# One of eight parts of a depthwise convolution made by ScalarE and GpSimd instead of VectorE, and one input projection issued earlier on TensorE

## What is computed

```python
hs = rmsnorm(hidden_states, ln_in_w)                 # 1024 tokens x 256
x, z = split(hs @ in_proj_w.T)                       # 512 channels each
xc = silu(depthwise_conv1d(x, conv_w, taps=4) + conv_b)
dt, Bm, Cm = split(xc @ x_proj_w.T, [128, 144])      # the "small" projection, 160 columns
dt = softplus(rmsnorm(dt) @ dt_proj_w.T + dt_proj_b)
# then a scan over the tokens: h = h * exp(dt * A) + dt * xc * B ;  y = sum(h * C)
```

## Time and profile before

| | us |
|---|---|
| median of 3 runs | 632.63 (631.25 to 633.44) |
| the profiled execution, its own time | 633.35 |
| its span, first to last instruction | 631.6 |
| busy PE / DVE / ACT / POOL | 587.5 / 467.1 / 387.2 / 300.3 |
| granted TensorE clock, mean | 0.988 |

### The profile page before, as it was taken

The page is one execution under the profiler, slowest core; times in us unless marked ns, Lnnn a source line. Parts: engine busy times, 40 slices in busy tenths (PEclk is TensorE's granted clock), DMA queues, the critical chain, the costliest instruction groups (busy, mean ns, idle before and its releaser), DMA issues.

```text
span 631.6 us, 10934 instructions
## 1 busy us (share of the span) xinstructions
PE 587.5 (93%) x3641; PEld 444.4 (70%) x3641; DVE 467.1 (74%) x788; ACT 387.2 (61%) x882; POOL 300.3 (48%) x242
## 2 busy tenths in 40 slices
PE   6999689998999999999999999999999999998874
PEld 3554589887998887597779779778855555665542
DVE  6989999999999967535463543553655789998885
ACT  5689899999999956522241231321755664687543
POOL 7022699999999991223333434344012332225101
PEclk9999899999999999999999999999999999999898
DMA  8001641211211117424440450411700000000002
GB/s 285 3 2 45 208 186 51 59 59 51 59 59 51 35 40 302 155 92 175 169 177 28 172 182 26 173 38 30 274 1 1 1 2 0 1 1 1 2 0 67
DMA packets 18261, 51.50 MB, mean 82 GB/s; under 512 B 3842, under 2 KB 9603, under 8 KB 16548
## 3 DMA queue, kind: packets, MB, share of 16 engines
q1 hardware_dynamic: 15172, 41.43, 18.5%
q0 software_dynamic: 2752, 7.34, 3.9%
q10 hardware_dynamic: 288, 2.10, 0.9%
HBM read 46.21 MB, written 4.66 MB: 81 GB/s over the span
## 4 chain that ended last, share of the span: by engine, by line
PE 67%; ACT 13%; DVE 10%; issue 5%; DMA 4%; SPq 0%; POOL 0%; POOLq 0%; DVEq 0%; ACTq 0%
PE ps L2174 11%; PE ps L2247 8%; ACT arena L689 7%; PE ps L2182 6%; PE ps L2236 4%; PE ps L2268 4%; ACT arena L704 3%; PE ps L1957 3%; PE ps L1942 3%; PE ps L1991 2%; PE ps L1783 2%; PE ps L2197 2%; PE ps L1792 2%; PE ps L1944 2%; DVE arena L1304 2%
## 5 line engine op out<-in xcount | busy, mean ns | idle before, releaser
L460 POOL TENSOR_TENSOR arena<-arena 128x1024 f32<-128x1024 f32 x63 | 147.3, 2393 | 3.4 <-DVE arena L1304 3.0
L1304 DVE TENSOR_TENSOR_SCAN arena<-arena,ps 128x1024 f32<-128x1024 f32 x64 | 143.4, 2279 | 4.0 <-ACT arena L689 0.9
L689 ACT ACTIVATE arena<-arena,a_neg 128x510 f32<-128x510 f32 x128 | 84.6, 710 | 1.9 <-DVE arena L1304 1.9
L2174 PEld LDWEIGHTS ps<-arena 128*128 128x128 f32 x660 | 75.5, 192 | 3.9 <-issue 3.1
L2174 PE MATMUL ps<-arena 128*128 128x128 f32 x660 | 77.2, 277 | 0.3 <-DVE arena L1481 0.3
L1942 PE MATMUL ps<-ident,arena 128*128 128x128 f32 x384 | 64.7, 278 | 9.9 <-ACT arena L700 8.6
L1957 PE MATMUL ps<-ident,arena 128*128 128x128 f32 x512 | 67.3, 274 | 2.5 <-DVE arena L1313 1.8
L900 ACT ACTIVATE arena<-ps 128x256 f32<-128x256 f32 x45 | 17.2, 383 | 83.0 <-PE ps L2174 83.0
L704 ACT ACTIVATE arena<-arena,b_tok 128x512 f32<-128x512 f32 x96 | 64.8, 710 | 0.0
L1957 PEld LDWEIGHTS ps<-ident,arena 128*128 128x128 f32 x512 | 57.8, 141 | 4.0 <-DVE arena L1313 1.3
L2247 PE MATMUL ps<-arena 128*128 128x512 f32 x128 | 58.2, 595 | 0.0
(11 more groups left out here) (317 smaller groups left out, 1147.2 us busy)
## 6 DMA issues: line engine op xcount, KB each, us to landing
arena<-in_w_moe SPq DMA_DIRECT2D x8, 2176.0 KB, 9.1
arena<-c_dram SPq DMA_DIRECT2D x32, 256.0 KB, 3.1
arena<-in_w_o ACTq DMA_DIRECT2D x1, 2048.0 KB, 12.7
arena<-in_w_qT SPq DMA_DIRECT2D x1, 2048.0 KB, 11.0
arena<-moe_out SPq DMA_DIRECT2D x8, 256.0 KB, 4.7
arena<-in_w_q SPq DMA_DIRECT2D x1, 2048.0 KB, 10.2
x<-in_x SPq DMA_DIRECT2D x2, 512.0 KB, 4.7
arena<-in_w_in SPq DMA_DIRECT2D x2, 512.0 KB, 6.5
```

The lines of the kernel that those rows point to most:

```text
L460: pool.tensor_tensor(in_chunks(hC[unit % 3]), in_chunks(h[unit % 3]), c_bc[:, m % C_BUFS, :].unsqueeze(1).to_broadcast([P, 2, HALF]), ALU. ...
L689: ins = nc.scalar.activation(dA_b[:, unit % 2, 2 * k:2 * k + 2, 1:], dt_b[:, c, 2 * half:2 * half + 2, 1:], ACT.Exp, scale=a_neg[:, c, n:n ...
L1304: nc.vector.tensor_tensor_scan(h[unit % 3], dA[:, k, :], ps[:, 2 * k:2 * k + 2, :].rearrange("p a b -> p (a b)"), 0.0, ALU.mult, ALU.add). ...
L2174: ins = nc.tensor.matmul(ps[:, bank, c * P:(c + 1) * P], w13[:, k, chunk * P:(chunk + 1) * P], xT[:, k, :], start=(k == 0), stop=(k == KD ...
```

## The change

Part (2, 0) of the convolution is taken out of DVE's list. ACT makes its four products instead (`multiply_taps`: Identity with the tap as a scale, three behind `take_in(2, 0)` and one behind `take_in(3, 0)`) into a new tile `tap_products`, which lies where the scan's rows `c_bc` are loaded later. POOL adds them up in three adds, between `negate_rates` and `rstd_of_dt(0)`, and ACT's `convolved(2, 0)` reads the sum. The last two chunks of the first half change places (3 before 2), for the Silu and for `project_small`. On PE `project_in(3, 1)` goes ahead of the four `project_small(., 0)`. On ACT `take_counts` goes ahead of the first `take_in`, `take_x(1)` ahead of `take_in(2, 0)`, and `take_in(3, 1)` ahead of `squares_of_small(0)`. Two semaphores are merged into one to make room for the new one, with the same waits.

```diff
+        tap_products = view(104.5, [TAPS, HALF])
-        CONV_TURNS = (((0, 0),), ((1, 0),), ((2, 0), (3, 0)), ((0, 1), (1, 1)), ((2, 1), (3, 1)))
+        CONV_TURNS = (((0, 0),), ((1, 0),), ((3, 0),), ((0, 1), (1, 1)), ((2, 1), (3, 1)))
+        SUMMED = (2, 0)
+        CHUNKS = ((0, 1, 3, 2), (0, 1, 2, 3))
+        convolved_at = lambda c, half: CI * half + CHUNKS[half].index(c) + 1
-        X_TAKEN, COUNTS_TAKEN = (1, 2), 3
+        X_TAKEN, COUNTS_TAKEN = (1, 3), 2
             negate_rates()
+            for k in range(1, TAPS):
+                pool.wait_ge(s["tap_products"], TAPS + k - 1)
+                pool.tensor_tensor(tap_products[:, 0, :], tap_products[:, 0, :], tap_products[:, k, :], ALU.add).then_inc(s["tap_products"], 1)
             rstd_of_dt(0)
+            def multiply_taps(*taps):
+                c, half = SUMMED
+                act.wait_ge(s["in_out"], CI * half + c + 1)
+                for k in taps:
+                    nc.scalar.activation(tap_products[:, k, :].rearrange("p (b t) -> p b t", b=2), xpad[:, c, 2 * half:2 * half + 2, k:k + SEQ], ACT.Identity,
+                                         scale=lane[:, c, LANE_AT["conv_w"] + k:LANE_AT["conv_w"] + k + 1]).then_inc(s["tap_products"], 1)
             def convolved(c, half):
-                act.wait_ge(s["conv_acc"], tap_added(c, half, TAPS - 1))
-                nc.scalar.activation(xc[:, c, halves[half]], conv[:, c, :], ACT.Silu,
+                if (c, half) == SUMMED:
+                    act.wait_ge(s["tap_products"], 2 * TAPS - 1)
+                else:
+                    act.wait_ge(s["conv_acc"], tap_added(c, half, TAPS - 1))
+                src = tap_products[:, 0, :] if (c, half) == SUMMED else conv[:, c, :]
+                nc.scalar.activation(xc[:, c, halves[half]], src, ACT.Silu,
             masks()
+            take_counts()
             take_in(0, 0)
             take_in(1, 0)
+            take_x(1)
             take_in(2, 0)
-            take_x(1)
+            multiply_taps(0, 1, 2)
             take_in(3, 0)
-            take_counts()
+            multiply_taps(3)
+            take_in(0, 1)
             convolved(0, 0)
-            take_in(0, 1)
             take_in(1, 1)
             convolved(1, 0)
             take_in(2, 1)
+            convolved(3, 0)
             convolved(2, 0)
-            convolved(3, 0)
+            take_in(3, 1)
             squares_of_small(0)
             take_small(0)
-            take_in(3, 1)
             convolved(0, 1)
             project_in(2, 1)
+            project_in(3, 1)
             project_small(0, 0)
             project_small(1, 0)
+            project_small(3, 0)
             project_small(2, 0)
-            project_small(3, 0)
-            project_in(3, 1)
             route_out()
             transpose_dt(0)
```

More of the change, by code:

```diff
@@ L228, in build @@
             gathered1 gathered2 gathered3 xT_psum xT_done gu_psum gate_act hid_done y_psum y_ready y_stored x1_sum waited
-            bn3 eps3 rstd_x1 x_normed ld_v ld_o ld_kq kv_psum kv_out k_squared
+            bn_x eps3 rstd_x1 x_normed ld_v ld_o ld_kq kv_psum kv_out k_squared
             k_ms masked k_rstd k_normed x1T_psum x1T_done q_psum q_squared q_eps q_rstd s_psum s_taken
             s_shifted s_exp s_soft pT_psum pT_done attn_psum attn_taken eps4 rstd_x2 ld_idx ld_late gathered_w0
-            gathered_w1 iota_done counted spread_psum spread_done quantised wT_psum wT_done x_scaled x_size_ready x_quant
+            gathered_w1 tap_products iota_done counted spread_psum spread_done quantised wT_psum wT_done x_scaled x_size_ready x_quant
             xT8_psum xT8_done ff_psum ff_read ff_gate ff_in t_scaled t_in_ready t_size_ready prod_done t_done t_psum
-            tT_done y2_psum y2_read bn5 eps5 rstd_out early_out out_shift stored""".split()
+            tT_done y2_psum y2_read eps5 rstd_out early_out out_shift stored""".split()
         s = {n: sem(n) for n in names}
@@ L1117, in convolve @@
                     if half:
-                        dve.wait_ge(s["conv_out"], c + 1)
+                        dve.wait_ge(s["conv_out"], convolved_at(c, 0))
                 for k in range(TAPS):
@@ L1200, in scan_inputs @@
                 dve.wait_ge(s["softplus"], n + 1)
-                dve.wait_ge(s["conv_out"], n + 1)
+                dve.wait_ge(s["conv_out"], convolved_at(c, half))
                 nc.vector.tensor_tensor(dtx[half][:, c, :], dt[:, c, halves[half]], xc[:, c, halves[half]], ALU.mult).then_inc(s["dtx_done"], 1)
@@ L1496, in variances @@
             def variances(stats, eps, tiles):
-                dve.wait_ge(s[stats], tiles.stop)
+                dve.wait_ge(s["bn_x"], stats + tiles.stop)
                 for i in range(tiles.start, tiles.stop):
@@ L1519, in add_results @@
                     dve.wait_ge(s["x1_sum"], 2 * part + i + 3)
-                    nc.vector.bn_stats(bn[:, i, :], x[:, i, :]).then_inc(s["bn3"], 1)
+                    nc.vector.bn_stats(bn[:, i, :], x[:, i, :]).then_inc(s["bn_x"], 1)
             def take_result_half(half):
@@ L1527, in _ @@
             add_results(1)
-            variances("bn3", "eps3", half_tiles[0])
+            variances(0, "eps3", half_tiles[0])
             add_results(2)
@@ L1533, in _ @@
             add_results(3)
-            variances("bn3", "eps3", half_tiles[1])
+            variances(0, "eps3", half_tiles[1])
             dve.wait_ge(s["rstd_x1"], 2)
@@ L1632, in add_result @@
                 dve.wait_ge(s["y2_read"], t + 1)
-                nc.vector.bn_stats(bn[:, t, :], x[:, t, :]).then_inc(s["bn5"], 1)
+                nc.vector.bn_stats(bn[:, t, :], x[:, t, :]).then_inc(s["bn_x"], 1)
             take_scores(0)
@@ L1731, in _ @@
             scale_of_hidden(7)
-            variances("bn5", "eps5", OUT_PARTS[0])
+            variances(TILES, "eps5", OUT_PARTS[0])
             add_result(6)
@@ L1737, in _ @@
             round_hidden(7)
-            variances("bn5", "eps5", OUT_PARTS[1])
+            variances(TILES, "eps5", OUT_PARTS[1])
             dve.wait_ge(s["rstd_out"], 2)
@@ L1741, in _ @@
             add_result(7)
-            variances("bn5", "eps5", OUT_PARTS[2])
+            variances(TILES, "eps5", OUT_PARTS[2])
             dve.wait_ge(s["rstd_out"], 3)
@@ L1800, in project_small @@
                         pe.wait_ge(s["routes_out"], 1)
-                pe.wait_ge(s["conv_out"], CI * half + c + 1)
+                pe.wait_ge(s["conv_out"], convolved_at(c, half))
                 for i in range(HALF_TILES):
@@ L1804, in project_small @@
                     ins = nc.tensor.matmul(ps[:, 2 * half + i // 2, (i % 2) * D:(i % 2) * D + XP], xc[:, c, tile * P:(tile + 1) * P], w_x[:, c, :],
-                                           start=(c == 0 and i % 2 == 0), stop=(c == CI - 1), skip_group_check=True)
+                                           start=(c == 0 and i % 2 == 0), stop=(c == CHUNKS[half][-1]), skip_group_check=True)
                 ins.then_inc(s["xproj_psum"], 1)
```

## The result

The changed kernel takes 635.06 us, median of 22 runs (632.6 to 638.2); the kernel before, run beside it, 632.68 (630.5 to 635.4, 22 runs). The ratio is 1.0036, 95% interval 1.0024 to 1.0048: the change costs 2.3 us (1.5 to 3.0). The forecast was 633.9, or +1.3.

A forecast was written before the change was run, and what follows sets the result against it. PE was taken to set the pace up to 62.5 us, then DVE. Removal and adds counted nothing; the move on PE left 1.75 us idle, net 1.3, so 632.63 + 1.3 = 633.9 us, range 631.0 to 636.3.

The forecast's parts named there:

- The hole: PE idles 1.75 us behind route_out before the transposes of dt at 34.01; some comes back, net 1.3 us later.
- the rival on the clock: PE's idle 1.75 us also drops the clock to half, costing 1.85 to 3.4 us more: 636.5 us; chance 0.18.
- The removal: DVE's 2.47 us less work becomes a wait before its turn (0,1), (1,1): worth nothing, a gain of at most zero.
- the rival by which DVE is the bound: DVE truly sets the pace, so a part less saves 2.47 us: 630.2 us; chance 0.13.
- the rival that nothing happens: The new order of PE's list is made up for elsewhere, as by hidden slack: 632.6 us; chance 0.16.
- the summed part: Rival: POOL's sum for (2, 0) comes late, PE waits at 29.4: 635 us or more; chance 0.03.
- The adds: POOL's three adds take 1.2 us each from 21.2 to 24.9, before ACT and PE need the sum: cost nothing.
- The size: Whole kernel: 1.3 us slower than the 632.63 median, giving 633.9 us.

The follow-up runs named there:

- the second execution: The changed kernel, unaltered, profiled once more: 635.84 us.
- the move alone: Kernel before with only project_in(3, 1) ahead of the four small projections on PE and take_in(3, 1) ahead of the squares on ACT: 634.02 us, ratio 1.0030.
- Without the adds: Changed kernel with POOL's three adds left out, so part (2, 0) holds the first tap's product only: 634.55 us, ratio 1.0042.
- the filled hole: Changed kernel with project_gates(0) moved behind route_out on PE and take_gates(0) moved forward on ACT: 634.18 us, ratio 1.0018.
- the old order: Changed kernel with project_in(3, 1) back behind the small projections on PE and take_in(3, 1) back behind take_small(0) on ACT: 634.50 us, ratio 1.0038.
- holding the clock: Four unread matmuls put into PE's 4.27 us wait: in the kernel before 631.17 us, ratio 0.9965; in the changed kernel 631.83, ratio 0.9982.
- the old order without the adds: Changed kernel with project_in(3, 1) and take_in(3, 1) put back and POOL's three adds left out, ACT's products kept: 632.50 us, ratio 1.0022.

## Why the prediction was right, and where not

**The hole: right.** PE idles 1.75 us before the first L1834, for DVE's scaling, behind `route_out`, and 0.45 comes back: 1.30 at `take_routing`, 1.28 in the second execution, and 1.29 with the move alone. The projections ended at 30.36, the transposes began at 33.91, `project_dt` at 35.65, each 0.1 ahead of the forecast, because this execution began 0.1 earlier. DVE's wait before the second mean squares shrank from 2.41 to 1.99, forecast about 0.4. The clock did not fall at this hole. (In the rival on the clock the prediction read "until about 74.5 us, some 3.7" from the earlier trace rows; the 0.96 of the window from 74 to 75 says 74.1 and 3.4. The forecast does not use it.)

**The removal: right.** Worth nothing. Without the adds DVE just waits 1.48 and 1.39 us, where it waits 0 and 0.17 with them. That refutes the rival by which DVE is the bound; the rival that nothing happens fell with the hole, and the summed part did not come late, as PE never waited for it. Where DVE does pace, the filled hole showed: at `take_routing`, 30 us farther on, not here.

**The adds: nothing for the sum, but not for the reason given.** "I take 1.2, since L460 reads two full tiles beside a busy DVE" priced the adds' own time, and "The adds cost nothing" looked only at who waits for POOL. They took 1.70 each. More than that, they took 2.8 us from DVE, more than the removed part's 2.47. I had cited the Trainium skill ("GPSIMD Engine Reference", Key points) on that contention and put no price on it; the rows here bear it out, with two-input operations on both sides. L460 with L1304 beside it could not price the pair, since nothing showed what either takes alone. With the old order this would have been a loss of 1.04 us, with the new one it hides behind the hole, 0.17 us short of showing.

**The size: 1.0 us short, and the cause of that is open.** The sum followed the path to `take_routing` and took the rest as a constant. It is not. After the wait of 4.27 us the clock falls in either kernel, and in the profiled execution of the changed one it stayed down for 6.8 us instead of 3.4, 1.0 us at the third scan. But the second execution of the changed kernel had the short stretch and was no faster, since the clock was at half again near the end. Whether the change makes the long stretch likelier is not settled: of its two traces one has it, of the two of before none, and its times run from 632.6 with a mean clock of 0.991 to 638.2 with 0.977. That holding the clock gives back more after the change (3.4 us) than before (2.2) points that way, but the intervals overlap. The mean granted clock over the whole span points the same way: 0.987 in the 22 runs of the changed kernel, 0.989 in the 88 of before that ran beside the experiments. The other part of the open 1.0 may be a cost behind the scans that the old order without the adds hints at. The Trainium skill ("TensorE: Matmul & The Clock Gate", Part 1) says of a kernel's start that how much runs at the low clock varies from run to run with the same kernel; at this later place the two traces of the changed kernel differ likewise (6.8 and 3.4 us).

## What to carry to other kernels

An add on POOL with two inputs was paid by DVE here, about 0.9 to 1.0 us for each: ask not only who waits for it, but what DVE has in hand meanwhile, and price it from a stretch where that pair runs. Before work is taken off an engine, find the wait in front of which it lies; if another engine ends that wait, the work was free. Where PE waits for several us in a phase that it paces afterwards, a few multiplications into a free bank can be worth more (here 2.2 us, 0.9 to 3.5) than a rearrangement. Before a difference of one or two microseconds is laid to one stretch of one trace, take a second trace of the same kernel: here the two of the changed one differed by 1.0 us at the third scan, and the other way round at the end.

## What the chip showed that I had not expected

- Beside three two-input adds of 128x512 on POOL, DVE's three `scalar_tensor_tensor` took 4.10 us instead of 2.33, its two `tensor_scalar`, with a single tensor input, 1.88 to 2.94 instead of 0.88; beside one-input operations the whole turn grew by 1.1 us, beside the adds by 3.1.
- A memset on POOL (1.80 us, no input at all) stretched a `tensor_scalar` on DVE from 0.48 to 2.23 us.
- Behind PE's wait of 4.27 us the granted clock came back after 3.4 or after 6.8 us at 1.2 GHz, in every trace one of the two. The wait was followed by a fall in every trace. Those of 1.75 us before the transposes brought none, that of 2.91 us did. The length of one wait alone doesn't tell: with the multiplications in, the clock fell at 79.75 us in the kernel before, behind a wait of 1.45 us and during one of 0.89, and did not fall at the same two waits in the changed one.
